# A graph network's layer with GRU gates: a new order of the four engines' queues within a step

## The reference

```python
mask = (adj[None] == labels[:, None, None, None])            # 4 labels
weight = mask / (sum(mask, -1, keepdims=True) + 1e-8)
agg = einsum('dbmn,bnh->bmdh', weight, hid)                  # -> b, m, 4 * 256
out = relu(agg @ Wd.T + bd)
r = sigmoid(out @ Wri.T + bri + hid @ Wrh.T + brh)
z = sigmoid(out @ Wzi.T + bzi + hid @ Wzh.T + bzh)
n = tanh(out @ Wni.T + bni + r * (hid @ Wnh.T + bnh))
h = (1 - z) * n + z * hid
result = (h - mean(h)) / sqrt(var(h) + 1e-5) * gamma + beta
```

## Time and profile before

| | us |
|---|---|
| median of 3 runs | 566.2 |
| lowest, highest | 565.68, 566.47 |
| the profiled execution | 565.02 |
| its span, first to last instruction | 563.2 |
| TensorE busy (matmuls) | 518.4 (92%) |
| VectorE busy | 466.9 (83%) |
| ScalarE busy | 412.2 (73%) |
| GpSimd busy | 365.6 (65%) |

### The profile page before, as it was taken

How to read it: one execution, slowest core, us unless ns; L and a number is a source line. 1 busy time by engine, 2 the same in 40 slices (tenths; PEclk the granted TensorE clock), 3 DMA queues, 4 the chain that set the end, 5 groups by cost and what they waited for, 6 DMA issues and landing times.

```text
span 563.2 us, 10546 instructions
## 1 busy us (share of the span) xinstructions
PE 518.4 (92%) x2951; PEld 438.6 (78%) x2951; DVE 466.9 (83%) x1077; ACT 412.2 (73%) x791; POOL 365.6 (65%) x368
## 2 busy tenths in 40 slices
PE   7987889999999999999999999999999999999993
PEld 4776777887787878788788778788788788878892
DVE  5897758888889888888988888888888898888887
ACT  5837777787787787677777778778778777777872
POOL 2967566676776676676676676667667667666435
PEclk9998999999999999999999999999999999999997
DMA  8111022111122111112211112111112210211111
GB/s 305 60 46 48 29 76 67 43 51 51 54 67 65 61 32 65 37 65 65 65 31 62 44 58 65 65 50 43 64 39 65 65 65 28 65 37 38 38 40 56
DMA packets 20261, 33.42 MB, mean 59 GB/s; under 512 B 2256, under 2 KB 6992, under 8 KB 20240
## 3 DMA queue, kind: packets, MB, share of 16 engines
q1 hardware_dynamic: 19872, 32.38, 17.5%
q10 hardware_dynamic: 288, 0.52, 0.3%
q0 software_dynamic: 80, 0.26, 0.1%
HBM read 24.77 MB, written 8.39 MB: 59 GB/s over the span
## 4 chain that ended last, share of the span: by engine, by line
DVE 40%; PE 27%; issue 15%; ACT 7%; POOL 7%; DMA 1%; DVEq 1%; ACTq 0%; POOLq 0%
PE alpha L410 11%; PE p_bank L447 6%; PE gamma L410 5%; PE y_bank L410 5%; DVE ratio L1487 4%; DVE shared L1497 4%; DVE mix L1508 4%; DVE masks L1177 4%; DVE shared L1513 3%; DVE y_lo L1490 3%; ACT shared L1042 3%; DVE mix L1462 3%; ACT shared L1047 2%; DVE out_rows L1449 2%; DVE out_rows L1446 2%
## 5 line engine op out<-in xcount | busy, mean ns | idle before, releaser
L447 PE MATMUL p_bank<-y_hi,masks 128*128 128x256 f32 x256 | 75.4, 316 | 16.2 <-POOL y_lo L1874 9.8
L995 ACT ACTIVATE p_bank<-p_bank,ratio 128x256 f32<-128x256 f32 x112 | 45.5, 444 | 55.7 <-PE p_bank L447 55.7
L1860 POOL TENSOR_TENSOR shared<-x_rows,shared 128x512 f32<-128x512 f32 x28 | 35.9, 1284 | 65.3 <-ACT shared L1042 65.3
L447 PEld LDWEIGHTS p_bank<-y_hi,masks 128*128 128x128 f32 x256 | 48.3, 189 | 38.1 <-DVE out_rows L1449 16.4
L447 PE MATMUL p_bank<-y_lo,masks 128*128 128x256 f32 x256 | 66.6, 282 | 0.0
L1852 POOL TENSOR_TENSOR x_lo<-x_f,x_hi 128x1024 fp32r<-128x1024 f32 x27 | 64.9, 2402 | 1.2 <-ACT x_hi L1008 1.2
L410 PE MATMUL alpha<-wx_hi,x_hi 128*128 128x384 f32 x122 | 47.2, 387 | 13.4 <-ACT shared L1047 12.0
L1843 POOL TENSOR_TENSOR var_eps<-mean_var,ln_eps 128x2 f32<-128x2 f32 x27 | 5.3, 197 | 82.2 <-DVE mean_var L1473 82.2
L410 PEld LDWEIGHTS alpha<-wx_hi,x_hi 128*128 128x128 f32 x122 | 22.9, 188 | 38.3 <-ACT shared L1047 23.9
L447 PEld LDWEIGHTS p_bank<-y_lo,masks 128*128 128x128 f32 x256 | 48.7, 190 | 0.1
L1446 DVE SCALAR_TENSOR_TENSOR out_rows<-p_bank,rcount,bd_rows 128x256 f32<-128x256 f32 x56 | 25.7, 458 | 26.6 <-PE p_bank L447 26.6
(11 more groups left out here) (311 smaller groups left out, 1866.6 us busy)
## 6 DMA issues: line engine op xcount, KB each, us to landing
x_f<-in_xT SPq DMA_DIRECT2D x32, 256.0 KB, 2.6
x_rows<-in_x SPq DMA_DIRECT2D x32, 256.0 KB, 2.6
out<-shared SPq DMA_DIRECT2D x31, 256.0 KB, 2.0
adj_in<-in_adjT SPq DMA_DIRECT2D x32, 128.0 KB, 2.0
shared<-in_wgT SPq DMA_DIRECT2D x2, 576.0 KB, 6.2
shared<-in_wdT ACTq DMA_DIRECT2D x2, 256.0 KB, 5.2
vec_rows<-in_vectors SPq DMA_DIRECT2D x1, 512.0 KB, 6.4
shared<-in_wgT SPq DMA_DIRECT2D x2, 192.0 KB, 6.9
```

Source lines behind the costliest of these rows:

```text
L447: last = nc.tensor.matmul(p_bank[:, b * H:(b + 1) * H], masks[:, k % 2, g, d, :], part[:, g, d * H:(d + 1) * H], start=first, stop=(part i ...
L995: nc.scalar.activation(p_bank[:, b * H:(b + 1) * H], p_bank[:, b * H:(b + 1) * H], ACT.Copy, scale=ratio[:, k % 2, g, b:b + 1]).then_inc(p ...
L1860: nc.gpsimd.tensor_tensor(from_n[:, :], x_rows[:, m % 2, :, :].rearrange("p g f -> p (g f)"), n_sb[:, :], ALU.subtract).then_inc(from_read ...
```

## The change

All of it is in the fast steps and the tail. The arithmetic is the same, in the same precision; no matmul is added or dropped.

The new orders in a step (a prime marks work of the pair before, which was done in the step before until now):

- TensorE: YP1, GP4', PF1', YP6, GP3', YP2, PS1, YP7, YP5, GP1, CNT, YP4, YP3, GP6, TRN, GP5, PF0, GP7, GP2, PS0.
- ScalarE: YSEED, C21', ASEED, SCALE1, U2Y, XHI, YH11, U3Y, SIG, BSEED, YH22, YH21, GSEED, U2, TANH, RELU, OHI, YH12, SCALE0, U3, C11, OSH.
- VectorE: mask 1, MIX, mask 2, statistics, mask 3, centres, C12', LAB1 first half, NORM, YL11, Y22, LAB1 second half, counts, mask 0 of pair i + 1, reciprocal, ratio, RN, PRE, YL21, Y12, sums of out, OLO, C22, LAB0.
- GpSimd: XSUM, roots, OLS', XLO, YL22, FROM, ZP, YL12.

The ratio was rcount times counts, both in SBUF; it is now (count in PSUM + 1e-8) times rcount in one instruction. TRN waits for the ratio in place of the counts. YH11 waits for `p_done` as well. The core of the diff (ScalarE's part is its order above):

```diff
 # TensorE, fast_step
                 y_product(y_alpha, A11, B11, True).then_inc(yp1_done, 1)
-                pe.wait_ge(alpha_loaded, up(q + 1))
-                pe.wait_ge(olo_ready, up(q + 1))
-                product(alpha, A11, B11).then_inc(p1_done, 1)
                 if n >= 2:
-                    pe.wait_ge(masks_ready, up(D * (i + 1), D))
-                    pe.wait_ge(olo_ready, up(i - 1))
-                    counted(i)
-                pe.wait_ge(p_scaled, up(4 * i, 4))
-                p_products(i - 1, 1, True)
+
+                    pe.wait_ge(u3_ready, up(q - 1))
+                    product(q - 1, alpha, A22, T4).then_inc(p4_done, 1)
+                    pe.wait_ge(yl11_ready, up(n - 1))
+                    pe.wait_ge(yl12_ready, up(n - 1))
+                    pe.wait_ge(out_ready, up(2 * i - 1, 2))
+                    p_products(i - 1, 1, False)
                 pe.wait_ge(y11_seeded, up(n))
                 if n == 1:
                     pe.wait_ge(wdt_ready, 3)
                 y_product(y_alpha, S2, T2).then_inc(yp6_done, 1)
+                if n >= 2:
+                    pe.wait_ge(c22_ready, up(q))
+                    product(q - 1, gamma, S4, B22).then_inc(p3_done, 1)
                 y_product(beta, A12, B21).then_inc(yp2_done, 1)
-                pe.wait_ge(gamma_loaded, up(q + 1))
-                pe.wait_ge(oslo_ready, up(q))
-                product(gamma, S1, T1).then_inc(p5_done, 1)
-                pe.wait_ge(out_ready, up(2 * i, 2))
-                pe.wait_ge(counts_ready, up(i + 1))
-                transposes()
+                pe.wait_ge(p_scaled, up(4 * i, 4))
+                p_products(i - 1, 1, True)
                 pe.wait_ge(u2y_ready, up(n))
...
-                pe.wait_ge(beta_seeded, up(q + 1))
-                product(alpha, S2, T2).then_inc(p6_done, 1)
-                product(beta, A12, B21).then_inc(p2_done, 1)
+                pe.wait_ge(alpha_loaded, up(q + 1))
+                pe.wait_ge(olo_ready, up(q + 1))
+                product(q, alpha, A11, B11).then_inc(p1_done, 1)
+                if n >= 2:
+                    pe.wait_ge(masks_ready, up(D * (i + 1), D))
+                    counted(i)
...
-                pe.wait_ge(u2_ready, up(q))
-                product(alpha, S3, T3).then_inc(p7_done, 1)
                 pe.wait_ge(y22_ready, up(n))
                 y_product(y_gamma, S4, B22).then_inc(yp3_done, 1)
+                pe.wait_ge(beta_seeded, up(q + 1))
+                pe.wait_ge(oslo_ready, up(q))
+                product(q, alpha, S2, T2).then_inc(p6_done, 1)
+                pe.wait_ge(out_ready, up(2 * i, 2))
+                pe.wait_ge(ratio_ready, up(i + 1))
+                transposes()
+                pe.wait_ge(gamma_loaded, up(q + 1))
+                product(q, gamma, S1, T1).then_inc(p5_done, 1)
                 pe.wait_ge(yl21_ready, up(n))
                 pe.wait_ge(yl22_ready, up(n))
-                pe.wait_ge(out_ready, up(2 * i, 2))
                 p_products(i, 0, False)
-                pe.wait_ge(u3_ready, up(q))
-                product(alpha, A22, T4).then_inc(p4_done, 1)
+                pe.wait_ge(u2_ready, up(q))
+                product(q, alpha, S3, T3).then_inc(p7_done, 1)
+                product(q, beta, A12, B21).then_inc(p2_done, 1)
                 pe.wait_ge(p_scaled, up(4 * i + 2, 4))
                 p_products(i, 0, True)
...
 # TensorE, tail
+                pe.wait_ge(u3_ready, q - 1)
+                product(alpha, A22, T4, q - 1).then_inc(p4_done, 1)
+                pe.wait_ge(yl11_ready, YPAIRS)
+                pe.wait_ge(yl12_ready, YPAIRS)
+                pe.wait_ge(out_ready, 2 * PAIRS - 1)
+                p_products(last, 1, False)
+                pe.wait_ge(c22_ready, q)
+                product(gamma, S4, B22, q - 1).then_inc(p3_done, 1)
...
 # ScalarE, fast_step: the added wait
                 act.wait_ge(yp2_done, up(n))
+
+                act.wait_ge(p_done, up(2 * i, 2))
                 nc.scalar.activation(y_hi[:, ODD, half(0)], beta[:, :], ACT.Copy).then_inc(yh11_ready, 1)
...
 # VectorE, fast_step: one mask at a time, and the ratio
+                def mask(k, d):
+
+                    dve.wait_ge(adj_loaded[k % 2], up(16 * (k // 2 + 1), 8))
+                    dve.wait_ge(p_done, up(2 * k - 2, 2))
+                    nc.vector.tensor_scalar(*label_masks(k, d)).then_inc(masks_ready, 1)
...
-                nc.vector.tensor_tensor(ratio[:, i % 2, :, :], rcount[:, i % 2, :, 0:4:2],
-                                        counts[:, i % 2, :, 1:4:2], ALU.mult).then_inc(ratio_ready, 1)
...
+                nc.vector.scalar_tensor_tensor(ratio[:, i % 2, :, :],
+                                               t_bank[:, 0:2 * D].rearrange("p (g d) -> p g d", g=2)[:, :, 1:4:2], EPS,
+                                               rcount[:, i % 2, :, 0:4:2], ALU.add, ALU.mult).then_inc(ratio_ready, 1)
...
 # GpSimd, fast_step
+                if n == 1:
+                    sum_blocks(i + 1, up, 16 * ((i + 1) // 2 + 1))
+                if has_pair(i + 2):
+
+                    sum_blocks(i + 2, up, up(16 * ((i + 2) // 2 + 1), 8))
                 if n >= 2:
                     pool.wait_ge(mv_ready, up(2 * j + 2, 2))
...
+                    pool.wait_ge(oshi_ready, up(i - 1))
+                    pool.wait_ge(p3_done, up(i - 3))
+                    nc.gpsimd.tensor_tensor(*split_lo(o_lo[:, i % 2, 3:7, :], o_sums[:, 1:5, :], o_hi[:, i % 2, 3:7, :]))\
+                        .then_inc(oslo_ready, 1)
```

More of the change, by code:

```diff
@@ L1002, in fast_step @@
                 nc.scalar.activation(beta[:, :], y_alpha[:, :], ACT.Copy).then_inc(y11_seeded, 1)
+                if n >= 2:
+                    act.wait_ge(p4_done, up(q))
+                    act.wait_ge(pre_ready, up(q - 1))
+                    act.wait_ge(rz_ready, up(q - 1))
+                    nc.scalar.activation(c_sb[:, EVEN, 0, :], alpha[:, :], ACT.Copy).then_inc(c21_ready, 1)
+                    act.wait_ge(c21_ready, up(q))
+                    nc.scalar.activation(alpha[:, :], vec_rows[:, 0:512], ACT.Copy).then_inc(alpha_loaded, 1)
+                scale(i - 1, 1)
+                act.wait_ge(yp6_done, up(n))
+                if n >= 2:
+                    act.wait_ge(yl12_ready, up(n - 1))
+                nc.scalar.activation(u2_y[:, :], y_alpha[:, :], ACT.Copy).then_inc(u2y_ready, 1)
                 if has_pair(i + 1):
@@ L1039, in fast_step @@
                 nc.scalar.activation(u3_y[:, :], y_alpha[:, :], ACT.Copy).then_inc(u3y_ready, 1)
+                for ready in (c11_ready, c21_ready, c22_ready, c12_ready):
+                    act.wait_ge(ready, up(m + 1))
+                act.wait_ge(zpart_ready, up(m))
+                act.wait_ge(rn_ready, up(m))
+                nc.scalar.activation(rz_sb[:, :, :, :], c_sb[:, :, :, 128:GATE], ACT.Sigmoid).then_inc(rz_ready, 1)
+                act.wait_ge(p1_done, up(q + 1))
+                act.wait_ge(yl11_ready, up(n))
+                nc.scalar.activation(beta[:, :], alpha[:, :], ACT.Copy).then_inc(beta_seeded, 1)
+                act.wait_ge(y22_ready, up(n))
+                nc.scalar.activation(y_hi[:, EVEN, half(1)], u3_y[:, :], ACT.Copy).then_inc(yh22_ready, 1)
+                act.wait_ge(yp4_done, up(n))
+                nc.scalar.activation(y_hi[:, EVEN, half(0)], y_alpha[:, :], ACT.Copy).then_inc(yh21_ready, 1)
+                act.wait_ge(c12_ready, up(q))
+                nc.scalar.activation(gamma[:, :], bias_step[:, :], ACT.Copy).then_inc(gamma_loaded, 1)
+                act.wait_ge(p6_done, up(q + 1))
+                nc.scalar.activation(u2_sb[:, :], alpha[:, :], ACT.Copy).then_inc(u2_ready, 1)
                 act.wait_ge(pre_ready, up(m + 1))
@@ L1107, in end_tanh @@
                     nc.scalar.activation(end_n[:, g, :], end_pre[:, g, :], ACT.Tanh).then_inc(end_n_ready, 1)
+                evict(EVEN, alpha, p4_done, c21_ready, last - 2)
                 act.wait_ge(p_first, 2 * PAIRS)
@@ L1113, in tail @@
                                          scale=ratio[:, last % 2, 1, b:b + 1]).then_inc(p_scaled, 1)
+                act.wait_ge(c21_ready, last - 1)
+                nc.scalar.activation(alpha[:, :], vec_rows[:, 0:512], ACT.Copy).then_inc(alpha_loaded, 1)
                 act.wait_ge(c12_ready, last - 1)
@@ L1462, in fast_step @@
                     nc.vector.tensor_tensor(mix[:, :], z_part[:, :], n_sb[:, :], ALU.add).then_inc(mix_ready, 1)
-                    dve.wait_ge(p_done, up(2 * i - 2, 2))
-                    make_masks(i, up(16 * (i // 2 + 1), 8))
+                    mask(i, 2)
                     dve.wait_ge(mix_ready, up(j + 1))
@@ L1503, in fast_step @@
                     nc.vector.tensor_tensor(*split_lo(lo, wd_sum_of[T4], hi)).then_inc(wdt_ready, 1)
+                dve.wait_ge(yh11_ready, up(n))
+                nc.vector.tensor_tensor(*split_lo(y_lo[:, ODD, half(0)], beta[:, :], y_hi[:, ODD, half(0)]))\
```

(24 more changed lines are left out.)

170 lines of the change are left out of this document (61 added, 109 removed).

## The result

The changed kernel takes 527.0 us (526.4 to 528.3, 4 runs) against 566.2 of the kernel before: ratio 0.9312, 95% interval 0.9291 to 0.9332, so 39 us or 6.9% faster. The profiled execution took 528.25, span 526.5.

The account below looks back on a forecast made before the run. The prediction took TensorE as near its limit, at 14.71 us a step; 14.71 + 0.44 + 0.72 = 15.87 against 16.68 gained 21.1 us over 26 periods, less 1 for the tail: 546.1 us, range 521 to 562.

Parts of the forecast that it names:

- a forecast with two blocks: TensorE stalls before YP3 (0.44 us) and before PF0 (0.72) in each step; chance 0.43.
- RN wins its race: Rival: VectorE's RN starts before GpSimd's YL22, so 0.72 us is not paid; step 15.15, 527.4 us; chance 0.23.
- 0.44 us for Y22: TensorE's YP3 waits for VectorE's late Y22, starting at 8.78 in place of 8.46, plus 0.12: 0.44 us lost.
- The sum for a step, 15.87: One step: TensorE's 14.71 us plus 0.44 before YP3 plus 0.72 before PF0, against 16.68 before.
- What bounds the kernel: TensorE is near its limit: it needs 14.71 us a step, 14.75 unhindered; some 1.9 us of each old step are stalls.
- The ratio stands behind x_lo: VectorE's ratio waits for GpSimd 1.4 us every step; reading PSUM, it takes 0.2 us in place of 1.57.
- What the moved products buy: On TensorE, GP4, GP3 and PF1 in the next step gain distance, a good us after their input; no work added.
- The first loss at the port: Mask 1, MIX and mask 2 run beside GpSimd's three x_f sums: VectorE loses 1.33 us, bounds 1.0 and 1.8.
- The margin: VectorE ahead of YP3: Y22 ends at 7.40 without port waits, YP3 wants it at 8.41, 1.0 us to spare.
- The race: After Y22, GpSimd's YL22 starts 0.3 us ahead of VectorE's RN and holds the port, delaying YL21 and PF0.
- the 0.72: TensorE's wait before PF0 for YL21, which comes late behind RN: 0.60 + 0.12 us a step.
- The tail: After the last step, ScalarE's work between GP4 and GP1 costs 0 to 2 us, taken as 1.

Follow-up runs that it names:

- the ratio alone: The kernel before with only the new ratio, which reads the counts in PSUM, transposes waiting for it, all orders old: 552.6 us, ratio 0.9754.
- the order alone: The changed kernel with the old ratio instruction (two SBUF inputs, no PSUM): 528.4 us, ratio 0.9328.
- YH21 ahead of YH22: The changed kernel with YH21 moved ahead of YH22 in ScalarE's order: 517.7 us, ratio 0.9144.

## Why the prediction was right, and where it was wrong

The range (521 to 562) held the 527.0 and the sign was right. The predicted time, 546.1, was that of a forecast with two blocks; the measured time is that of the rival "RN wins its race", 527.4, though not by its mechanism. RN loses in 18 of 24 steps, and that the two numbers meet is luck: the rival paid 0.44 us for Y22 and nothing for the race, the kernel pays nothing for Y22 and 0.38 for the race. The sum for a step, 15.87, comes to the measured one when its terms are put right: 15.87 - 0.44 (Y22) - 0.34 (race) + 0.15 (TensorE's own work) = 15.24. These periods are 17 of the 19 us between forecast and result; most of the rest is that the profiled execution of before was 1.2 us under its median and that of the changed kernel 1.2 over.

**What bounds the kernel:** right. TensorE's need was put at 14.71 us a step, or 14.75 with nothing in its way; the kernels that TensorE alone sets take 14.86, and so do the steps of the changed kernel in which RN wins (14.86 to 14.90 from YP1 to YP1).

**The ratio stands behind x_lo:** right, 1.57 to 0.15. That only a part of it is on the loop I had not said in the prediction; *the ratio alone* gave 0.53 us a step, and *the order alone* showed that the new place would have done for it too.

**What the moved products buy:** right that it buys time (I had given it no size), wrong in reason for GP4 and GP3. I wrote that each comes a good us after its own input. The run with both moved back shows that their inputs were in time there too; their worth is the 1.04 us of work that each puts between YP1 and YP6, and between PF1 and PS1, while ScalarE makes YSEED and SCALE1. For PF1 the reason held, the distance from the sums that it waits for: without it PF1 waits 1.3 us in nearly every step and the kernel is 32 us slower. LAB0 comes last there, with YL12 0.3 us ahead of it.

**The first loss at the port:** this is the step of the prediction that failed, in its size and in what it would cost. I took 1.33 us from four masks in a row beside GpSimd; it was 0.73 in the step read. I misread that row. Its first mask stood behind another GpSimd instruction, `wo_lo`, which ran until 53.80, and not behind a sum:

```profile
51.81 1.99 POOL L1745 TENSOR_TENSOR wo_lo<-shared,wo_hi 128x384 fp32r<-128x384 f32 x2
```

```profile
53.14 0.81 DVE L1177 TENSOR_SCALAR masks<-adj_in 128x256 fp32r<-128x256 int32 x1
```

The next mask began 0.73 us later in place of 0.20, so 0.53 of the 1.33 belong to `wo_lo`, and 0.8 to the three sums, close to the 0.73 here. The margin was mis-sized too. Y22 ends at 306.52, 7.85 us into the step (YP1 at 298.67) in place of 8.73: 0.6 by the smaller loss, 0.3 by handovers that I placed too late. YP3 starts at 8.58. So the whole loss fits into the time to spare (even 1.33 would have ended Y22 at 8.45, just ahead of YP3), YP3 waits in no step, and the 0.44 of the sum vanish. *YH21 ahead of YH22* shows this, with masks nearly as slow and a step of 14.86.

**The race:** right in place and winner, off in size. I had YL22 0.3 us ahead of RN; it is some 0.08 in most steps. YH22 starts at 306.94 behind BSEED (306.45 to 307.03), not at Y22's end (306.52) + 0.04 as I placed it. BSEED had waited for TensorE (0.19 us here), and YL22 starts 8.96 to 8.98 us into every step, while RN comes at 8.90 to 9.33, by what the masks and MIX lost before it. A quarter of the steps win. A step that loses costs less than the 0.72: PF0 was due at 310.50 (one matmul spacing, 0.17, behind the last of GP5 at 310.33) and began at 310.89, with its second matmul 0.11 later still than in a free run: 0.5. 18 x 0.5 / 24 = 0.38, and 14.86 + 0.38 = 15.24, against 15.21 measured. From YP1 to YP1 a step that loses takes 15.34 to 15.38 and one that wins 14.86 to 14.90, which is the same 0.5.

**The tail:** 1 us taken, 1.5 measured for head and tail together.

What stays open: why the race goes one way in three steps of four. The trace shows where it starts. In the step ahead of each of the six wins GpSimd's FROM starts 0.07 to 0.08 us behind TANH's end; ahead of 17 of the 18 losses it is some 0.22. GpSimd's x_f sums then come 0.13 earlier than in the step read, mask 1 takes 0.31 to 0.34 in place of 0.46, and RN comes at 8.90 to 8.94. Why FROM is sooner once in four steps, the length of a round of the loop, is not known, and no run tested it. Nor was every part of the new order tested by itself: GP7 no longer waits for U2 and GP6 no longer for BSEED, and no run put GP7, GP6 or ScalarE's order back.

## What to carry to other kernels

Give each two-input SBUF instruction of VectorE, and each tensor-scalar from SBUF to SBUF like the masks, a place where GpSimd is idle or where its loss is covered, and check the margin. Here a race lost by 0.1 us in most steps cost 9 us, and one swap on a third engine settled it. A wait that costs nothing where it stands can still decide a race behind it. Before a row is taken as a price, see which instruction each part of it waited for. A product moved between two others is worth what it covers for them, whether or not its own input is early. Two edits that each reach the bound alone may make a new loop together.

## What the runs showed of the hardware

- A 4-element instruction with two SBUF inputs took 0.15 to 0.16 us free and 1.57 behind GpSimd's x_lo; with one input in PSUM it took 0.15 in the same order, at 302.80, in the middle of x_lo (301.94 to 304.34).
- The wait goes both ways, and the winner is whoever is there first, by as little as 0.03 us (277.38 against 277.41). The loser's time grows by most of the winner's duration: RN from 0.70 to 1.79 behind a YL22 of 1.31, YL22 from 1.31 to 1.83 behind an RN of 0.70. The Trainium skill (SBUF — State Buffer, section "Who interferes with whom") says that whoever issues first gets the shared pair for the whole instruction; by that rule, these rows agree.
- When the two came level while a mask still ran, VectorE went first: GpSimd's second sum and MIX both start at 300.17, and MIX goes through at 0.69 while the sum takes 1.27. In all 18 of the 24 steps in which their recorded starts lie within 0.01 us it went so. When the sum stood ahead, also while a mask ran (284.73 against 284.85), the sum went first, with 0.80 against MIX's 1.24.
